# Routing a two-expert layer on raw rows and a centred router, with one engine making the rows and the list's one-hots carrying tile numbers

## What is computed

```python
# third layer (relational); x is (3125, 256), agg the summed messages, deg the edge counts
n = layernorm(x)
x = x + relu(n @ self_W + self_b + agg / clip(deg, 1))
# fourth layer (experts); N = 3125, E = 8
tokens = layernorm(x)                      # (x - m) / sqrt(v + 1e-5)
logits = tokens @ router_w.T
probs  = softmax(logits)
rw, re = top_k(probs, 2)
rw     = rw / max(rw.sum(-1), 1e-12)
out    = tokens
for e in range(8):
    h   = gelu(tokens @ w1[e] + b1[e])
    out = out + combine[:, e:e+1] * (h @ w2[e] + b2[e])   # combine holds rw at re
x = x + out
```

## Time and profile before

| | us |
|---|---|
| median of three runs | 1973.9 |
| lowest and highest | 1972.54, 1975.08 |
| the profiled execution | 1972.32 |
| its span in the trace | 1970.6 |
| last message summed, router stage begins | at 1694.2 |
| last logits matmul ends, softmax begins | at 1752.5 |
| first gather of the expert stage | at 1784.3 |
| last scatter of the expert stage begins | at 1928.3 |

### The profile page before, as it was taken

The page is one execution under the profiler, slowest core; times in us unless marked ns, Lnnn a source line. Parts: engine busy times, 40 slices in busy tenths (PEclk is TensorE's granted clock), DMA queues, the critical chain, the costliest instruction groups (busy, mean ns, idle before and its releaser), DMA issues.

```text
span 1970.6 us, 22614 instructions
## 1 busy us (share of the span) xinstructions
PE 1431.9 (73%) x6252; PEld 937.2 (48%) x6252; DVE 1305.9 (66%) x2938; ACT 575.1 (29%) x1687; POOL 1373.6 (70%) x1383
## 2 busy tenths in 40 slices
PE   5666477788888887579999966677676777457970
PEld 3333256655655555457784433334333333246860
DVE  6999878798888887485993044544444444666544
ACT  0687411156666662132333300000000000342320
POOL 0788577777777777778877277777777777546771
PEclk9799788889999999789999989988767667557995
DMA  5111143445544444602004563333333333312337
GB/s 93 12 31 28 33 106 104 108 118 132 136 117 115 129 106 106 74 1 63 2 1 116 150 206 104 106 106 104 105 106 105 104 105 103 48 47 78 101 104 214
DMA packets 105416, 183.74 MB, mean 93 GB/s; under 512 B 31178, under 2 KB 69533, under 8 KB 105170
## 3 DMA queue, kind: packets, MB, share of 16 engines
q0 software_dynamic: 56384, 134.58, 27.6%
q1 hardware_dynamic: 47603, 45.16, 8.5%
q10 hardware_dynamic: 1308, 2.56, 0.5%
HBM read 151.56 MB, written 30.38 MB: 92 GB/s over the span
## 4 chain that ended last, share of the span: by engine, by line
POOL 34%; PE 25%; DVE 19%; issue 13%; DMA 7%; ACT 1%; DVEq 1%; SPq 0%; POOLq 0%; ACTq 0%
POOL gath L898 32%; DVE hot_c L641 6%; PE ps L932 6%; PE ps L1321 4%; DMA gath<-y_tab,index_b 4%; PE ps L1283 4%; PE ps L1269 3%; DVE hot_r L632 2%; PE ps L1710 2%; PE ps L1721 2%; DMA wide<-y_nodes 1%; DMA gath<-h_tab,index_a 1%; DVE acc L923 1%; POOL y_nodes L1682 1%; DVE gath L971 1%
## 5 line engine op out<-in xcount | busy, mean ns | idle before, releaser
L932 PE MATMUL ps<-gath,hot 128*125 128x260 f32 (+1 forms) x1808 | 615.6, 476 | 296.0 <-DVE gath L971 108.0
L932 PEld LDWEIGHTS ps<-gath,hot 128*125 128x125 f32 x1808 | 354.1, 221 | 517.3 <-DMA gath<-y_tab,index_b 196.8
L898 POOL DMA_INDIRECT gath<-h_tab,index_a x464 | 447.6, 965 | 150.0 <-issue 138.4
L898 POOL DMA_INDIRECT gath<-y_tab,index_b x440 | 417.4, 949 | 166.8 <-issue 123.2
L923 DVE TENSOR_TENSOR acc<-acc,ps 125x257 f32 (+1 forms) x672 | 284.0, 423 | 328.4 <-PE ps L932 299.1
L673 PE MATMUL ps<-hot_c,pay 125*128 125x440 f16 (+1 forms) x901 | 194.4, 369 | 63.9 <-ACT pay L662 59.7
L728 POOL DMA_INDIRECT slot_tab_b<-sent_word_b,sent_to_b x136 | 165.0, 1213 | 36.3 <-issue 36.3
L718 POOL DMA_INDIRECT slot_tab<-sent_word,sent_to x102 | 130.4, 1279 | 82.3 <-DVE sent_to L480 51.5
L662 ACT ACTIVATE pay<-hot_r,plan_b 125x128 f16<-125x128 f16 x578 | 172.0, 386 | 0.0
L673 PEld LDWEIGHTS ps<-hot_c,pay 125*128 125x128 f16 x901 | 87.7, 101 | 162.3 <-ACT pay L662 81.2
L971 DVE TENSOR_TENSOR gath<-gath,ps 128x1024 f32<-128x1024 f32 x116 | 135.9, 1212 | 0.0
(11 more groups left out here) (330 smaller groups left out, 2026.6 us busy)
## 6 DMA issues: line engine op xcount, KB each, us to landing
y_tab<-ybuf SPq DMA_DIRECT2D x25, 448.0 KB
gath<-h_tab,index_a POOLq DMA_INDIRECT x464, 2.8
gath<-y_tab,index_b POOLq DMA_INDIRECT x440, 2.8
h_tab<-hbuf SPq DMA_DIRECT2D x25, 113.8 KB
xa<-in_x SPq DMA_DIRECT2D x1, 2800.0 KB
xa<-in_x SPq DMA_DIRECT2D x5, 560.0 KB
xn_tab<-acc SPq DMA_DIRECT2D x25, 112.0 KB
out<-xa SPq DMA_DIRECT2D x5, 560.0 KB
```

What stands on the lines that cost most here:

```text
L898: p.indirect_dma_start(gath[:, ring(k) + s, 0:width], None, table, bass.IndirectOffsetOnAxis(ap=index[g][:, col:col + 1], axis=0)).then_in ...
L932: ins = t.matmul(ps[0:NP, 4 + q % 2, 0:width], hot[:, s, :], gath[:, s, 0:width], start=(e == 0), stop=(e == n - 1))
```

## The change

`x3 = xa + relu(xb)` is now made by DVE alone, in one more instruction per tile behind each "third". PE transposes these rows `xa` and not the normed ones, and multiplies them by a router whose rows had their mean subtracted, so that the node's mean drops out; the node's positive factor `rstd` leaves the order of its logits as it is, and is multiplied in only for the softmax. The statistics are taken over all 25 tiles at once, the norm's rows are made by ACT behind the logits' copies. The router is centred and turned inside the third layer, at groups 30 and 31 of its 55.

The residual `xa + norm(xa)` is made by ACT in the first 25 steps of the expert stage, as `xa * (rstd + 1) + nmr`. Top two work on the logits; softmax is needed for the weights only, and `route_weights`, with the softmax's division, follows `moe_vector`. The one-hot rows carry the tile's number plus one (`KTH * k + t + 1`) in place of one, the one-hot columns stay bare, and the row number is found by a division (`held`, `place_f`). The scatters' `dest_i` is released by a second step of `moe_ready`.

```diff
@@ relation_vector, relation_scalar, relation_tensor
+    def center_router(v):
+        v.wait_ge(moe_in, MOE_IN)
+        v.tensor_reduce(r_mean[:, :], r_s[:, :], AX, ALU.add).then_inc(vector_step, vn.up())
...
+        v.tensor_scalar(r_s[:, :], r_s[:, :], r_mean[:, 0:1], None, ALU.add).then_inc(router_centered, 1)
...
+            if k == ROUTER_GROUP:
+                center_router(v)
...
+            if k == ROUTER_GROUP + 1:
+                t.wait_ge(router_centered, 1)
+                for c in range(2):
+                    ins = t.transpose(ps[:, 0, c * EXP:(c + 1) * EXP], r_s[:, c * 128:(c + 1) * 128], ident[0:EXP, 0:EXP])
+                ins.then_inc(rs_turned, 1)
@@ route_pool
-        for t in range(NT):
-            p.wait_ge(third_relu, t + 1)
-            p.tensor_tensor(flat(xa, t), flat(xa, t), flat(xb, t), ALU.add).then_inc(x3_made, 1)
-        for t in range(NT):
-            p.wait_ge(x_normed, TURN["moe"] + t + 1)
-            p.tensor_tensor(flat(xa, t), flat(xa, t), acc_cols(t, D), ALU.add).then_inc(x_added, 1)
-        p.wait_ge(er_col, 2)
-        p.tensor_tensor(hot_ec[:, 1, :, 1, :], hot_raw[:, 1, :, :], spread(tile_id[:, 1, :], MOE_TILES), ALU.mult).then_inc(er_tile, 1)
@@ route_scalar
+        for t in range(NT):
+            a.wait_ge(x_turned, TURN["moe"] + t + 1)
+            if t >= U5:
+                a.wait_ge(logit_made, t - U5 + 1)
+            a.copy(xt[:, t % U5, :, :], route_turn(t).rearrange("p (k n) -> p k n", k=2)).then_inc(xt_copied, 1)
+        a.wait_ge(var_ready, 6)
+        a.activation(tmp25[:, :], var[:, :], ACT.Sqrt).then_inc(root_done, 1)
+        a.wait_ge(norm_ready, 6)
         for t in range(NT):
+            a.activation(acc_cols(t, D), flat(xa, t), ACT.Identity, bias=nmr[:, t:t + 1], scale=rstd[:, t:t + 1]).then_inc(x_normed, 1)
+        for k in range(2):
+            a.wait_ge(er_col, k + 1)
+            a.mul(hot_ec[:, k, :, 0, :], hot_ec[:, k, :, 1, :], row_id[:, 0:1]).then_inc(er_row, 1)
         a.wait_ge(logit_ready, 1)
         a.activation(prob[:, :, :], logit[:, :, :], ACT.Exp).then_inc(prob_exp, 1)
+        a.activation(first_root[:, :], ones[0:1, 0:1], ACT.Gelu)
@@ route_tensor
-                t_eng.wait_ge(x_normed, TURN["moe"] + t + 1)
+                t_eng.wait_ge(x3_made, t + 1)
...
-                    ins = t_eng.transpose(route_turn(t)[:, k * NP:(k + 1) * NP], acc[:, t * AW + k * 128:t * AW + (k + 1) * 128], ident[0:NP, 0:NP])
+                    ins = t_eng.transpose(route_turn(t)[:, k * NP:(k + 1) * NP], xa[:, t, k * 128:(k + 1) * 128], ident[0:NP, 0:NP])
@@ route_vector
+        third(0)
+        for t in range(NT):
+            if t + 1 < NT:
+                third(t + 1)
+            v.wait_ge(third_summed, t + 1)
+            v.scalar_tensor_tensor(flat(xa, t), flat(xb, t), 0.0, flat(xa, t), ALU.max, ALU.add).then_inc(x3_made, 1)
+        for t in range(NT):
+            v.wait_ge(x3_made, t + 1)
+            ins = v.bn_stats(stats[:, t, :], flat(xa, t))
+        ins.then_inc(vector_step, vn.up())
+        v.wait_ge(vector_step, vn.n)
+        norm_sums(v, every)
+        v.wait_ge(pool_ready, IOTAS)
+        v.wait_ge(logit_made, NT)
+        for k, (left, most) in enumerate(((logit_p, s1), (comb[:, :, :], s2))):
+            v.tensor_reduce(most[:, :], left, AX, ALU.max).then_inc(vector_step, vn.up())
+            if k == 0:
+                norm_scale(v, 6, every)
...
+        v.tensor_tensor(logit[:, :, :], logit_p, b8(s1), ALU.subtract).then_inc(vector_step, vn.up())
...
+        v.tensor_scalar(sum_scale[:, :], rstd[:, :], 1.0, None, ALU.add)
+        v.tensor_tensor(logit[:, :, :], logit[:, :, :], b8(rstd), ALU.mult).then_inc(logit_ready, 1)
...
-            v.tensor_tensor(hot_raw[:, k, :, :], iota_r[0:NP, 0:MOE_TILES].unsqueeze(1).to_broadcast([NP, NT, MOE_TILES]),
-                            spread(slot_col[:, k, :], MOE_TILES), ALU.is_equal).then_inc(er_col, 1)
-        v.wait_ge(er_col, 2)
-        v.tensor_tensor(hot_ec[:, 0, :, 1, :], hot_raw[:, 0, :, :], spread(tile_id[:, 0, :], MOE_TILES), ALU.mult).then_inc(er_tile, 1)
+            v.tensor_tensor(hot_ec[:, k, :, 1, :], iota_r[0:NP, 0:MOE_TILES].unsqueeze(1).to_broadcast([NP, NT, MOE_TILES]),
+                            spread(slot_col[:, k, :], MOE_TILES), ALU.is_equal).then_inc(er_col, 1)
...
-                ins = v.tensor_scalar(hot_er[:, k * NT + t, :], iota_r[0:NP, :], slot_row[:, k, t:t + 1], None, ALU.is_equal)
+                ins = v.tensor_scalar(hot_er[:, k * NT + t, :], iota_r[0:NP, :], slot_row[:, k, t:t + 1], float(KTH * k + t + 1),
+                                      ALU.is_equal, ALU.mult)
...
+        v.tensor_scalar(held[:, :], tiles, 1.0, None, ALU.max).then_inc(vector_step, vn.up())
+        v.wait_ge(vector_step, vn.n)
+        v.reciprocal(held[:, :], held[:, :]).then_inc(vector_step, vn.up())
...
+        v.tensor_scalar(node_i[:, :], node_f[:, :], -float(NP + 1), 0.0, ALU.add, ALU.max).then_inc(moe_ready, 1)
@@ moe_pool
         for u in range(MOE_BODY):
             gather_x(u)
+        p.wait_ge(moe_ready, 2)
@@ moe_scalar
+            if u < NT:
+                a.activation(flat(xa, u), flat(xa, u), ACT.Identity, bias=nmr[:, u:u + 1], scale=sum_scale[:, u:u + 1]).then_inc(x_added, 1)
@@ vector
             route_vector(v)
+            moe_vector(v)
             route_weights(v)
-            moe_vector(v)
```

More of the change, by code:

```diff
@@ L247, in build @@
     s1, s2 = (end.tile(n, [NP, NT]) for n in ("s1", "s2"))
-    tile_id, row_id = end.tile("tile_id", [NP, 2, NT]), end.tile("row_id", [NP, 1])
-    node_f, kth, empty, dump, dest_f = (end.tile(n, [128, MOE_TILES]) for n in ("node_f", "kth", "empty", "dump", "dest_f"))
+    row_id = end.tile("row_id", [NP, 1])
+    r_mean = end.tile("r_mean", [EXP, 1])
+    sum_scale = end.tile("sum_scale", [NP, NT])
+    node_f, kth, held, place_f, empty, dump, dest_f = (end.tile(n, [128, MOE_TILES]) for n in ("node_f", "kth", "held", "place_f", "empty", "dump", "dest_f"))
     dest_i, node_i = (end.tile(n, [128, MOE_TILES], I32) for n in ("dest_i", "node_i"))
@@ L1399, in relation_scalar @@
             a.copy(xt[:, 0, :, :], ps[:, 0, 0:2 * NP].rearrange("p (k n) -> p k n", k=2)).then_inc(xt_copied, 1)
+        a.wait_ge(rs_turned, 1)
+        a.copy(r_t[:, :, :], ps[:, 0, 0:2 * EXP].rearrange("p (k e) -> p k e", k=2)).then_inc(rt_copied, 1)
+        a.activation(first_root[:, :], ones[0:1, 0:1], ACT.Sqrt)
     def relation_tensor(t):
@@ L1484, in route_tensor @@
     def route_tensor(t_eng):
         t_eng.wait_ge(moe_in, MOE_IN)
-        for k in range(2):
-            ins = t_eng.transpose(ps[:, 0, k * EXP:(k + 1) * EXP], r_s[:, k * 128:(k + 1) * 128], ident[0:EXP, 0:EXP])
-        ins.then_inc(rs_turned, 1)
         t_eng.wait_ge(rt_copied, 1)
@@ L1535, in route_vector @@
         v.wait_ge(self_added, NT)
-        def third(i):
-            for t in range(i * U5, (i + 1) * U5):
-                v.scalar_tensor_tensor(flat(xb, t), acc_cols(t, D), s2[:, t:t + 1], flat(xb, t), ALU.mult, ALU.add).then_inc(third_summed, 1)
-        for i in range(AHEAD):
-            third(i)
-        for i in range(SETS):
-            for t in range(i * U5, (i + 1) * U5):
-                v.wait_ge(x3_made, t + 1)
-                ins = v.bn_stats(stats[:, t, :], flat(xa, t))
-            ins.then_inc(vector_step, vn.up())
-            v.wait_ge(vector_step, vn.n)
-            norm_sums(v, set_of(i))
-            if i + AHEAD < SETS:
-                third(i + AHEAD)
-            norm_scale(v, 6 + i, set_of(i))
@@ L1562, in route_vector, with third @@
-        v.tensor_tensor(prob[:, :, :], prob[:, :, :], b8(s2), ALU.mult).then_inc(vector_step, vn.up())
-        v.wait_ge(vector_step, vn.n)
-        v.wait_ge(pool_ready, IOTAS)
-        for k, left in enumerate((prob, comb)):
-            v.tensor_reduce(s1[:, :], left[:, :, :], AX, ALU.max).then_inc(vector_step, vn.up())
-            v.wait_ge(vector_step, vn.n)
-            v.tensor_tensor(top[:, :, :], left[:, :, :], b8(s1), ALU.is_equal).then_inc(vector_step, vn.up())
+        def third(t):
+            v.scalar_tensor_tensor(flat(xb, t), acc_cols(t, D), s2[:, t:t + 1], flat(xb, t), ALU.mult, ALU.add).then_inc(third_summed, 1)
@@ L1569, in route_vector @@
+        v.wait_ge(pool_ready, IOTAS)
[4 more added lines that the diff above has]
+                norm_scale(v, 6, every)
+            v.wait_ge(vector_step, vn.n)
+            v.tensor_tensor(top[:, :, :], left, b8(most), ALU.is_equal).then_inc(vector_step, vn.up())
             v.wait_ge(vector_step, vn.n)
@@ L1630, in route_vector @@
         v.wait_ge(vector_step, vn.n)
[L1631 removed]
+        v.reciprocal(held[:, :], held[:, :]).then_inc(vector_step, vn.up())
+        v.tensor_scalar(kth[:, :], tiles, float(KTH), None, ALU.is_ge)
         v.wait_ge(vector_step, vn.n)
[L1633 removed]
+        v.tensor_tensor(place_f[:, :], rows, held[:, :], ALU.mult).then_inc(vector_step, vn.up())
@@ L1635, in route_vector @@
```

(12 more changed lines are left out.)

80 lines of the change are left out of this document (21 added, 59 removed).

## The result

| | before | after |
|---|---|---|
| median of the runs, us | 1973.8 (1972.54 to 1975.08, 4 runs) | 1941.79 (1940.55 to 1942.55, 4 runs) |
| the profiled execution | 1972.32 | 1942.26 |
| its span | 1970.6 | 1940.5 |

The account below looks back on a forecast made before the run. POOL's gathers and scatters were taken to bound the expert stage, so the first gather's time counts: 24.8 (rows and logits) + 5.9 (logits to gather) = 30.7 us off 1972.3 gives 1941.6, plus 1.6 for the median: 1943, range 1939.5 to 1950.

Parts of the forecast that it names:

- (a): Logits to gather: top two begin at once, without the softmax steps ahead of them; net 1.8 us gained.
- (b): Logits to gather: three instructions on the tiles' experts move into a later wait for PE; 0.4 us gained.
- (c): Logits to gather: the product with the tile number goes, and one-hot rows run 0.163 us apart; 3.9 us gained.
- (d): Logits to gather: the list gets a reciprocal and two more steps, but the gather leaves `dest_i` behind; 0.2 us lost.
- the second operation: One-hot rows now also multiply by a constant: taken as zero cost, at most 54 ns each, 2.7 us kept for the range.
- What is late next: ACT's later norms and SP's 50 stores: landed by 1752 at the latest, 1.6 us ahead of the list's release.
- What is worth nothing: Expert stage: moved `route_weights`, ACT's 25 additions to `xa` and the second wait on `moe_ready` don't change the time.
- (1): Rival: stores at the slower burst's pace come last, the gather is 4 us late, 1947 us; 12%.
- (2): Rival: the store queue backs up, up to 1.65 us per DMA, 50 stores need 82 us; 2003 us, slower; 3%.
- (3): Rival: TensorE's clock rises in the gapless stretch, DVE becomes the bound, 0.8 us more gained; 1942 us; 8%.
- (4): Rival: ACT, not POOL, slowed the thirds; at 0.78 each only 12.9 us are gained; 1961 us; 5%.
- (5): Rival: POOL's expert-stage pace comes from PE's tiles, so an earlier list is of no use; no change; 1%.

Follow-up runs that it names:

- warm: Changed kernel plus unread 464-column f16 matmuls on PE, six ahead of the first row tile and one beside each tile; 1939.49 us, ratio 0.9825.
- list_only2: Kernel before with only the new list (bare columns, rows carrying the tile's number, division, gather behind node_i), on another chip; 2246.79 us beside 2251.66 there.
- stores_twice: Changed kernel with each tile's normed rows stored a second time, first into a table nobody reads, 100 stores for 50; 1962.79 us, ratio 0.9945.
- act_twice: Changed kernel with a second idle 125x256 ACT activation beside each of the 25 residual additions in the expert stage; 1941.54 us, ratio 0.9838.

## Why the prediction was right

The forecast was 1943 us, and 1941.79 came. By its steps:

- **What bounds the kernel.** Held on the chips that ran the two kernels compared. Gather to end is 186.0 us after 186.3 worked out, in all kernels there 185.4 to 186.8, whatever was done before the gather or beside it. It did not hold on the other chip, where POOL did wait for `y_done` (signalled with `y_buf`), one of the signs named for being wrong, and the same stretch took 217.2 and 220.6 us.
- **Rows and logits, 24.8 us.** Held: 55.95 - 31.21 = 24.74, PE as the releaser. Its parts were less exact than the sum. The instruction with a maximum and an add was priced like its neighbour, 0.41, and costs 0.33 (it also has a constant where the neighbour reads a column, and no run tells these two apart); DVE makes a tile in 0.73, the rows in 18.3 us in place of 20.5, and PE is the bound by 3.57 us, not by 0.8. That the error cost nothing is due to PE's being the bound; in warm, where it isn't, the 2.2 us between 20.5 and 18.3 are most of the 3.6.
- **From the logits to the gather, 5.9 us.** Held: 6.07. From the logits to the counts (L1582, now L1559) 7.32 became 5.29, 2.0 gained where (a) has 1.8 net. From the counts to the read of the node sums 22.55 became 18.33, 4.2 gained, which is (b) and (c) less the 0.1 that the subtraction shows; list_only2 confirms them apart from the rest. After that 1.93 became 2.11, the 0.2 lost of (d). The view of the one-hot rows in the changed kernel settles the second operation:

```profile
L1599 DVE TENSOR_SCALAR gath<-iota_r,slot_row x50: 245/247/247, 1743.4 to 1751.4; 125x128 f16<-125x128 f16 x50
```

  247 ns for 241, and the starts still 0.163 apart. So the 2.7 us that the range held for it were not needed.
- **What is late next.** Counted in the stage, ACT's norms begin at 1728.6 of before's time, as worked out, and take 12.4 us for 12.9; the 50 stores take 21.2 for 20.4, the traffic ends at 1751.8 for "1752 at the latest". One number of this part doesn't fit the forecast's own sum: one-hot rows that last until 1753 would leave 0.6 us to a gather at 1753.6, where the rows before show 2.7 from the last one-hot row (1781.6) to the gather. They end at 1750.6 of before's time (1751.6 here), and nothing else hung on that number. The margin is what the sum gave, 1.7 for 1.6 by the traffic, and 1.1 by stores_twice.
- **What is worth nothing.** Held for all three that were tried. ACT's additions cost 0.60 each, not the 0.51 taken, and the 14.8 us more of act_twice were hidden too. The second wait on `moe_ready` was not tried by itself; POOL shows no wait there.
- **The rivals.** (1) and (2) fell: 0.42 us per store over 50 and over 100, with no slower stretch. (3) fell for the changed kernel, whose clock stays at 0.50 with PE busy for 28 of 30 us; the Trainium skill's rule that sustained activity releases the throttle (TensorE: Matmul & The Clock Gate, "What's actually happening") is not what this trace shows. When the clock does rise, in warm, the gain is 3.6 us and not the 0.8 of the rival, by the mis-sized DVE tile. (4) fell, but not by the reading given against it: in the five thirds at 0.41 ACT's relu was idle as well as POOL, and of the fifteen at "0.78 each" the first three, with POOL not yet or just begun, are 0.40 apart and the others 0.87. What refutes it are thirds at 0.40 beside the relu alone, at 1696.98 and 1715.65 in the kernel before; with ACT copying beside them they go at 0.40 too. (5) fell: the kernel's end moved with the first gather.
- **The sum.** The profiled executions are 30.1 us apart, where 30.7 was worked out: 30.8 in the stage, and it began 1.0 later. The forecast added 1.6 for the distance of before's profiled execution from the median; after's stood 0.5 above its median, on the other side. These 2.1 us high, less the 0.6 by which the profiled executions lie closer together than the sum, are the forecast's error (1.2 us; 1.4 before rounding). They are the spread of runs and of the stage's start, not the kernel.

## What to carry to other kernels

When a stage ends with one small result that releases a long chain of fixed pace, cost the edit as what it moves that release, and find the other thing that it waits for, which comes due just ahead of it: here the stores, 1 to 2 us away. A node-wise affine step (mean, positive scale) can be folded into the constant operand and applied after the product, which takes a chain of three engines out of the wait; it was worth 24 us here, or 19 on top of the single engine, while a cheaper way to make the rows was worth 5 in the old order and about 1 in the new. Look for elementwise work on GpSimd beside VectorE: its own time may be hidden and still be paid for by VectorE.
